# A two-layer block of mixtures, convolution and LoRA experts: lora_a in one load of longer runs, one step of x loaded later, A loaded and transposed sooner

## The reference, cut to what matters

```python
def layer0(x, cond):                                   # added to x
    h   = gelu(gelu(cond @ W0 + b0) @ W1 + b1)
    att = softmax(h @ W2 + b2)                         # 128 x 8
    o   = einsum('boi,bih->boh', einsum('bk,koi->boi', att, weight), x) + (att @ bias_k)[:, :, None]
    logits = o @ Wr.T                                  # 4 experts, the best 2 gated by a softmax
    mid = einsum('tf,erf->ter', o, A)                  # A: 4 experts x 16 x 512
    return sum_e gates[e] * (mid[e] @ B[e].T) * SCALE

def layer1(x1, cond):                                  # added to x1
    o1  = conv1d(x1, weight, 9 taps, 4 groups) + (cond @ c_weight.T)[:, :, None] + bias
    g   = relu(layernorm(o1 @ gw1.T + gb1)) @ gw2.T + gb2   # 8 experts, the best 2, capacity over all rows
    tmp = einsum('ni,eir->enr', o1, lora_A)            # lora_A: 8 experts x 512 x 16
    return o1 @ W.T + einsum('enr,ero->no', tmp * w, lora_B) / 16
```

## Time and profile before

| what | value |
|---|---|
| median of 3 runs | 302.68 us |
| the profiled execution's own time | 302.07 us |
| its span | 300.3 us |
| granted TensorE clock, mean | 0.997 |
| busy share: PE, DVE, ACT, POOL | 96%, 65%, 42%, 32% |
| moved by DMA | 52.75 MB, 176 GB/s over the span |

### The profile page before, as it was taken

How to read it: one execution, slowest core, us unless ns; L and a number is a source line. 1 busy time by engine, 2 the same in 40 slices (tenths; PEclk the granted TensorE clock), 3 DMA queues, 4 the chain that set the end, 5 groups by cost and what they waited for, 6 DMA issues and landing times.

```text
span 300.3 us, 6135 instructions
## 1 busy us (share of the span) xinstructions
PE 288.7 (96%) x1982; PEld 236.5 (79%) x1982; DVE 195.4 (65%) x506; ACT 125.3 (42%) x263; POOL 95.1 (32%) x124
## 2 busy tenths in 40 slices
PE   7999979999999999999999999999999999999994
PEld 5788957687978797879877987798777876777883
DVE  1655964743669466946594749474948555899885
ACT  3325834434622572258224822392237326103430
POOL 4361425123311431143114311431113235217660
PEclk9999999999999999999999999999999999999998
DMA  5796699893869487946794669458646790005887
GB/s 142 186 339 143 154 252 233 212 213 75 220 185 210 87 218 211 178 93 181 228 189 104 161 224 207 104 154 204 129 104 163 187 206 6 0 2 188 320 331 280
DMA packets 74400, 52.75 MB, mean 176 GB/s; under 512 B 44405, under 2 KB 61477, under 8 KB 74377
## 3 DMA queue, kind: packets, MB, share of 16 engines
q1 hardware_dynamic: 72936, 51.37, 69.1%
q10 hardware_dynamic: 1120, 1.07, 1.1%
q0 software_dynamic: 320, 0.02, 0.2%
HBM read 35.67 MB, written 16.78 MB: 175 GB/s over the span
## 4 chain that ended last, share of the span: by engine, by line
PE 54%; DMA 14%; SPq 12%; DVE 8%; issue 5%; ACT 4%; POOL 1%; DVEq 0%; ACTq 0%
PE ps_g L1139 10%; PE ps_d L1139 9%; DMA xg<-x1d 8%; PE ps_c L1277 7%; DMA x1d<-xq 7%; PE ps_a L1100 5%; PE ps_t L1293 3%; SPq L353 3%; PE ps_a L1089 3%; SPq L356 2%; ACT xq L632 2%; PE ps_d L1318 2%; PE ps_d L1319 2%; PE ps_d L1500 1%; PE ps_d L1505 1%
## 5 line engine op out<-in xcount | busy, mean ns | idle before, releaser
L512 POOL TENSOR_TENSOR o1l<-o,o1h 128x512 fp32r<-128x512 f32 x30 | 39.4, 1313 | 150.2 <-ACT o L644 150.2
L1139 PE MATMUL ps_d<-wt_hi,o1h 128*128 128x336 f32 (+1 forms) x120 | 41.1, 342 | 0.3 <-DVE y_all L961 0.3
L1139 PE MATMUL ps_d<-wt_hi,o1l 128*128 128x336 f32 (+1 forms) x120 | 38.7, 323 | 0.0
L1139 PE MATMUL ps_d<-wt_lo,o1h 128*128 128x336 f32 (+1 forms) x120 | 38.6, 322 | 0.0
L1277 PE MATMUL ps_c<-xg,cw 96*32 96x512 f32 x256 | 34.1, 604 | 3.1 <-DMA xg<-x1d 3.1
L955 DVE TENSOR_TENSOR oT<-ps_c,biasT 128x512 f32<-128x512 f32 x32 | 21.9, 686 | 22.8 <-PE ps_c L1277 21.9
L1139 PE MATMUL ps_g<-wt_hi,o1h 128*128 128x336 f32 x112 | 35.6, 318 | 0.6 <-ACT tmp_all L659 0.4
L1139 PE MATMUL ps_g<-wt_hi,o1l 128*128 128x336 f32 x112 | 35.5, 317 | 0.0
L1139 PE MATMUL ps_g<-wt_lo,o1h 128*128 128x336 f32 x112 | 35.4, 316 | 0.0
L632 ACT ACTIVATE xq<-y_all 128x512 f32 (+1 forms) x29 | 31.9, 1152 | 7.3 <-DMA x1d<-xq 4.1
L1100 PEld LDWEIGHTS ps_a<-pm,xT 128*128 128x128 f32 x256 | 30.2, 192 | 1.4 <-issue 0.8
(11 more groups left out here) (258 smaller groups left out, 577.7 us busy)
## 6 DMA issues: line engine op xcount, KB each, us to landing
xg<-x1d SPq DMA_DIRECT2D x64, 254.0 KB, 5.1
xg<-x1d SPq DMA_DIRECT2D x32, 256.0 KB, 3.8
x1d<-xq SPq DMA_DIRECT2D x30, 256.0 KB, 3.6
xs<-in_x_dram SPq DMA_DIRECT2D x6, 1024.0 KB, 6.2
out_dram<-xT SPq DMA_DIRECT2D x16, 256.0 KB, 2.1
out_dram<-xg SPq DMA_DIRECT2D x15, 256.0 KB, 2.1
y_all<-in_x_dram ACTq DMA_DIRECT2D x2, 512.0 KB, 5.2
y_all<-in_x_dram SPq DMA_DIRECT2D x1, 1024.0 KB, 5.7
```

Of the source, the lines that this page charges most:

```text
L512: pool.tensor_tensor(lo, o1[t % 2][:, :, :], hi.bitcast(fp32), ALU.subtract).then_inc(s_o1l, 1)
L1139: last = T.matmul(bank[:, 0:columns], a[:, Q - 1 - q, :], w[:, q, first:first + columns], start=(q == 0 and n == 0), stop=(q == Q - 1 and ...
```

## The change

It alters no arithmetic. (1) lora_a is loaded in one transfer: four neighbouring rows lie on one partition in DRAM already, so a run is 4 x 16 numbers (256 bytes). For that `ga` is laid out as blocks of 16 columns by q by 16, and the four places that read or write it use views of that. (2) Step 3 of x is not loaded in the setup, but in step 1 of SP's list, like those of the later steps, between the writes of step 1 and gather (1,1). (3) A and Wr are loaded ahead of the mixture's weights; PE transposes them where a `keep_busy` stood, DVE copies them to `pm` before three other instructions, and u's second product moves ahead of the transposition of B.

```diff
--- before.py
+++ after.py
@@ -29,6 +29,7 @@
     ER1 = E1 * R1
     G1 = gw1.shape[0]
     GC = G1 + ER1
+    GB = G1 // R1
     MC = (H + GC) // 2
     TAPS = convw.shape[2]
     CG = convw.shape[1]
@@ -63,6 +64,9 @@
             shape = list(v.shape)
             shape[axis] = n
             return v.broadcast_to(shape)
+
+        def blocks(v):
+            return v.rearrange("p q (e r) -> p e q r", r=R1)
 
         def wait(eng, s, value):
 
@@ -92,7 +96,7 @@
         rs = sb("rs", [P, UC])
         b_hi = sb("b_hi", [P, H], fp32r)
         b_lo = sb("b_lo", [P, H], fp32r)
-        ga = sb("ga", [P, Q, GC])
+        ga = sb("ga", [P, GC // R1, Q, R1])
         cw = sb("cw", [P, G, Q, CG])
         gw2bd = sb("gw2bd", [P, NT, E1])
         ident = sb("ident", [P, P])
@@ -331,13 +335,13 @@
             sp.dma_start(w1n, w1).then_inc(s_ld["w1"], 16)
             sp.dma_start(ctxn, ctxw).then_inc(s_ld["ctx"], 16)
             sp.dma_start(w2n, w2).then_inc(s_ld["w2"], 16)
+            sp.dma_start(aw[0:ER0], ffa.rearrange("e r h -> (e r) h")).then_inc(s_ld["aw"], 16)
+            sp.dma_start(aw[ER0:UC], ffr).then_inc(s_ld["aw"], 16)
             sp.wait_ge(s_wk0, 1)
             for j in range(4):
                 sp.dma_start(wk[C * j:C * j + K0],
                              mixw.rearrange("k (o j) i a -> j k o (i a)", j=4)[j])\
                   .then_inc(s_ld["mixw"], 16)
-            sp.dma_start(aw[0:ER0], ffa.rearrange("e r h -> (e r) h")).then_inc(s_ld["aw"], 16)
-            sp.dma_start(aw[ER0:UC], ffr).then_inc(s_ld["aw"], 16)
             sp.dma_start(mbn, row(mixb, 1, BT)).then_inc(s_ld["mixb"], 16)
             for e in range(E0):
                 sp.dma_start(bn[:, :, e * R0:(e + 1) * R0],
@@ -346,15 +350,13 @@
             sp.dma_start(wn, wmain.rearrange("(c p) h -> p c h", p=P)).then_inc(s_ld["w"], 16)
             sp.dma_start(gw1n, gw1).then_inc(s_ld["gate"], 16)
             sp.dma_start(gw2n, row(gw2, 1, NT)).then_inc(s_ld["gate"], 16)
-            for i in range(2):
-                sp.dma_start(xs[i][:, :, :], x_v[2 + i]).then_inc(s_x[i], 16)
+            sp.dma_start(xs[0][:, :, :], x_v[2]).then_inc(s_x[0], 16)
+            sp.dma_start(ga[:, GB:, :, :].rearrange("p e q r -> p e (q r)"),
+                         lora_a.rearrange("e (m q) r -> m e (q r)", q=Q)).then_inc(s_ld["lora_a"], 16)
             sp.wait_ge(s_zero, 1)
             for i in range(Q):
                 sp.dma_start(taps[i:C:Q, :, 7 - i:7 - i + TAPS],
                              convw.rearrange("o c k -> c o k")).then_inc(s_ld["conv"], 16)
-            for e in range(E1):
-                sp.dma_start(ga[:, :, G1 + e * R1:G1 + (e + 1) * R1],
-                             lora_a[e].rearrange("(m q) r -> m q r", q=Q)).then_inc(s_ld["lora_a"], 16)
 
             def write(u, t):
 
@@ -401,7 +403,7 @@
                         sp.wait_ge(s_x1w[1], (s + 1) * 16)
                     else:
                         wait(sp, s_x1w[2], (s + 1) * 32)
-                if has(s, 2) and not at_step(s, 0) and not at_step(s, 1):
+                if has(s, 2) and not at_step(s, 0):
 
                     sp.dma_start(xs[par][:, :, :],
                                  x_v[bass.ds(s + 2, 1)].rearrange("s p t h -> p (s t) h")).then_inc(s_x[par], 16)
@@ -520,8 +522,8 @@
                     mixing(1)
                     pool.wait_ge(s_gah, 1)
                     pool.wait_ge(s_gm, 2)
-                    pool.tensor_tensor(wt_lo[:, :, H:H + GC], ga[:, :, :], wt_hi[:, :, H:H + GC].bitcast(fp32),
-                                       ALU.subtract).then_inc(s_gal, 1)
+                    pool.tensor_tensor(blocks(wt_lo[:, :, H:H + GC]), ga[:, :, :, :],
+                                       blocks(wt_hi[:, :, H:H + GC].bitcast(fp32)), ALU.subtract).then_inc(s_gal, 1)
                     o1_low(0, 0)
                     return
                 if has(s, 2):
@@ -705,8 +707,8 @@
                     gate0_exp(1)
 
                     act.wait_ge(s_ss["gw1"], 1)
-                    act.wait_ge(s_ld["lora_a"], 16 * E1)
-                    nc.scalar.activation(wt_hi[:, :, H:H + GC], ga[:, :, :], ACT.Copy).then_inc(s_gah, 1)
+                    act.wait_ge(s_ld["lora_a"], 16)
+                    nc.scalar.activation(blocks(wt_hi[:, :, H:H + GC]), ga[:, :, :, :], ACT.Copy).then_inc(s_gah, 1)
                     gm_out(1)
                     u_out(2)
                     o_hi(0, 0)
@@ -833,6 +835,8 @@
             link(V.reduce_sum(sm[:, 1:2], atte, AXX))
             link(V.reciprocal(sm[:, 2:3], sm[:, 1:2]))
             V.tensor_scalar(attw[:, :, 0:K0], row(atte, 1, 4), sm[:, 2:3], None, ALU.mult).then_inc(s_ss["att"], 1)
+            dve.wait_ge(s_sp["pm"], 1)
+            V.tensor_copy(pm[:, :, :].rearrange("p c u -> p (c u)"), ps_t[:, 0:HC * UC]).then_inc(s_ss["pm"], 1)
             dve.wait_ge(s_sp["ctx"], 1)
             dve.wait_ge(s_ld["side"], 16)
             V.tensor_tensor(bex.rearrange("n (g q o) -> n g q o", q=Q, o=CG),
@@ -842,8 +846,6 @@
             dve.wait_ge(s_const, 4)
             V.tensor_tensor(attD, row(ps_v[:, 0:N0], 1, 4), row(repmask[:, :], 2, N0), ALU.mult).then_inc(s_attD, 1)
             V.tensor_copy(attT, ps_v[:, 0:P]).then_inc(s_ss["attT"], 1)
-            dve.wait_ge(s_sp["pm"], 1)
-            V.tensor_copy(pm[:, :, :].rearrange("p c u -> p (c u)"), ps_t[:, 0:HC * UC]).then_inc(s_ss["pm"], 1)
             dve.wait_ge(s_ss["pm"], 1)
             V.reduce_sum(pmsum, pm[:, :, :].rearrange("p c u -> p u c"), AXX).then_inc(s_ss["pmsum"], 1)
 
@@ -970,7 +972,7 @@
                     for t in range(NT):
                         V.tensor_copy(gw2bd[G1 * t:G1 * t + G1, t, :],
                                       ps_v[G1 * t:G1 * t + G1, Q * G1:Q * G1 + E1])
-                    V.tensor_copy(ga[:, :, 0:G1], ps_v[:, 0:Q * G1].rearrange("p (q g) -> p q g", q=Q))\
+                    V.tensor_copy(ga[:, 0:GB, :, :], ps_v[:, 0:Q * G1].rearrange("p (q e r) -> p e q r", q=Q, r=R1))\
                      .then_inc(s_ss["gw1"], 1)
                     for j in (1, 3):
                         dve.wait_ge(s_mps, 2)
@@ -1186,25 +1188,24 @@
             pe.wait_ge(s_xf, 16)
             t1(0, xs_early[0], 0)
             t1(0, xs_early[0], 1)
-            keep_busy(1)
+            pe.wait_ge(s_ld["aw"], 32)
+            pe.wait_ge(s_attd, 1)
+            for c in range(HC):
+                last = T.transpose(ps_t[:, c * UC:(c + 1) * UC], aw[:, c * P:(c + 1) * P], ident[0:UC, 0:UC])
+            last.then_inc(s_sp["pm"], 1)
             pe.wait_ge(s_ss["att"], 1)
             T.transpose(ps_v[:, 0:P], attw.rearrange("p j k -> p (j k)"), idp).then_inc(s_sp["attT"], 1)
             pe.wait_ge(s_xh, 16)
             pe.wait_ge(s_xt, 1)
             t1(0, xs_early[0], 2)
-            pe.wait_ge(s_ld["aw"], 32)
-            for c in range(HC):
-                last = T.transpose(ps_t[:, c * UC:(c + 1) * UC], aw[:, c * P:(c + 1) * P], ident[0:UC, 0:UC])
-            last.then_inc(s_sp["pm"], 1)
             pe.wait_ge(s_xt, 2)
             t1(0, xs_early[0], 3)
             pe.wait_ge(s_ss["pm"], 1)
-            u_products(0, (0,))
+            u_products(0, (0, 1))
             pe.wait_ge(s_bn, 1)
             for c in range(HC):
                 last = T.transpose(ps_t[:, c * P:(c + 1) * P], bn2[:, c, :, :].rearrange("p d e -> p (d e)"), idp)
             last.then_inc(s_sp["b"], 1)
-            u_products(0, (1,))
             pe.wait_ge(s_attD, 1)
             pe.wait_ge(s_ss["wkr"], 1)
             for o in range(MO):
@@ -1304,7 +1305,7 @@
                     wait(pe, s_y, s * NT)
                     for q in range(Q):
                         last = T.matmul(ps_g[:, 0:GC], o1[t % 2][:, Q - 1 - q, :],
-                                        ga[:, q, :], start=(q == 0), stop=(q == Q - 1))
+                                        ga[:, :, q, :], start=(q == 0), stop=(q == Q - 1))
                     last.then_inc(s_gp, 1)
 
                 def delta(u, t):
```

## The result

The change runs in 307.12 us (median of 20 executions, 303.32 to 315.66, and a single one of 1566 us that nothing here explains). The kernel before, on the same chip, has 302.17 (20 executions, 299.74 to 306.3). The ratio is 1.0151, with a 95% interval of 1.0111 to 1.0191. The forecast was 301.5, the range 299.4 to 303.3, and "slower by over 1%" had a chance of 0.04. (The ratios here leave out executions far above the quickest of their kernel; the medians don't.)

A forecast was written before the change was run, and what follows sets the result against it. PE, open 96% of the span, was taken as the bound, so only its waits count. Gain 2.9 us at conv (1,0), 1.7 given back at conv (1,1): 1.2 off 302.07 is 300.9, plus 0.61 gives 301.5; range 299.4 to 303.3.

The forecast's parts named there:

- The setup queue: SP's setup list: one lora_a load instead of eight frees SP near 24 to 26 us, needed by 27.9 for write (0,0).
- The head: Before the mixture by u: transposing A sooner brings that product (19.11) forward by 0.85 us, bounds 0 and 1.05.
- 0, if A or B lands late: Lower bound on the 0.85 us gain at the mixture by u: nothing gained when either load arrives late.
- conv (0,0): PE's first conv: with write (0,0) at 27.9, its 1.97 us wait goes; start 37.1 instead of 39.95, gain 2.85.
- The gates were late next: Step 1's gates end at 39.4, PE comes at 39.1; transposition at 39.5, gain 2.4; conv (0,1) at 42.4.
- Step 1: Gather (1,0) 3.7 us earlier, conv (1,0) gains 2.9; gather (1,1) lands at 63.15, PE waits 1.7, conv (1,1) gains 1.2.
- The 2.8: Delay in us that the moved 1 MB x load adds to gather (1,1), from 1.05 MB at 378 GB/s.
- the bound of 6.0: Upper bound in us on the x load's delay of gather (1,1), if nothing overlaps; as a rival 304.7 us, 10%.
- the clock falls: Rival: PE's clock halves in the first microseconds, where a matmul of ones goes, costing 4 us: 305.5; chance 2%.
- the 0.6 that I had added for the median: Added to the sum's 300.9: the median of the runs shown lies 0.61 us above the profiled 302.07.

## Why the prediction was wrong, step by step

*The setup queue: right, with more room than one of its reasons gives.* SP was free at 24.11, before 27.9, and write (0,0) went when its data came. But the taps took 10.26 us as they had 10.23, with 1 MB less and lora_a's load ahead of them; with 1 MB less and nothing in its place (x moved alone) they took 9.61. So the megabyte is worth little there. In the kernel with lora_a alone they end at 28.0, and that is early enough too.

*The head: wrong, +0.85 forecast, -0.2 measured.* "A is transposed before 9.2" took the load as 3 us sooner there because it was issued 3 us sooner. It had waited for that load in the kernel before as well, 0.19 us at 10.16, a row that I hadn't read. The bound "0, if A or B lands late" was the case, and below it lay a small loss that I had not put in.

*conv (0,0): right.* 38.11 for 37.1; the missing microsecond is the head's. The gates were late next, as forecast: PE waits 0.31 us for them, and conv (0,1) runs at 43.45 for 42.4.

*Step 1: conv (1,0) gained 1.9 for 2.9, and the gather (1,1) landed at 65.38 for 63.15.* This is the sum's error, and the terms can be read off. Gather (1,0) was issued 2.4 us sooner than before, not 3.7 (51.17 for 53.57), since both things that it waits for, write (1,0), landed at 51.11, and conv (0,2), done at 50.95, came later than I had them: 1.3 us. From there to the last part of gather (1,1), SP's own issues, that of x among them, took 0.65 more of the lead (56.20 for 57.95). The 1 MB made the landing 9.18 - 6.1 = 3.1 longer, where I took 2.8. In all 2.2 us, and 65.38 it is. In this execution, the quickest of its 20, the price of the load was nearly right and the queue's lead was not. But the last part of gather (1,1) took 8.29, 9.18, 10.15 and 11.26 us to land in the four profiles with the load, so the load's price runs from 2.2 to 5.2 us over the 6.1 of before. The 2.8 was near the low end of that, and the bound of 6.0 nearer than I weighed it.

*The clock: the step that failed.* The prediction charged the wait at conv (1,1) with its length, 1.7 us. I had a rival "the clock falls", but put it in the head, where PE transposes, and gave it 2%; at the one place where I myself forecast PE idle for 1.7 us, I did not ask for it. In 17 of 19 executions (the one of 1566 us aside) the mean clock shows a fall, and the median lies 3.8 us over those that kept it. Filling the wait brought 3.1 us back and the clock with it. No execution of the change with a fall was profiled; the two profiles with the same load that have one show it at conv (1,1), at 3.0 and 1.9 us, the second with a gather 2.2 us later besides. So about 3 of the 3.8 us are the clock, and the rest is most likely a longer wait. The miss adds up: 2.2 for the landing, 0.2 behind it, 3.8 between the two levels, less the 0.6 that I had added for the median, is 5.6, and 301.5 + 5.6 = 307.1.

*What stood in plain sight:* the first three times of before, 301.27 to 303.99, lay 2.7 us apart, with the profiled one at 302.07. I read that as noise. It was the same mechanism: a wait at conv (0,0), up to 2 us and more, with a fall behind it in some executions. In 99 executions of before beside the experiments, 37 had a clock of 0.996 or more and took 299.6 to 302.2 us, the rest 303.0 to 309.3. The profiled 302.07, from which the sum starts, is at the slow end of the first kind: only one of the 37 was slower. So the gain of lora_a's load is 2.4 us by the profiles (302.07 - 299.7), near the 2.0 that the forecast's terms leave without A's 0.85; but that this agrees is in part luck, since it counts from an execution that was slow for its kind. Between executions that kept the clock it is 0.55 and 1.15 us (medians, in the two groups on one chip), and by the medians of all it is 4.6: the part that I had not seen is the clock again.

## What to carry to other kernels

Price a wait of the TensorE not by its length alone: where it is as long as those behind which these profiles show a fall (1.92 to 5.08 us), add what the fall would cost, here 1.9 to 3.0 us, and look for it wherever the change creates a wait and wherever it removes one. Don't put a large load into a queue ahead of a transfer that is just in time: 1 MB ahead of a gather with 0.3 us to spare cost 2.5 to 5 us of idle PE. Nor need an earlier issue be an earlier landing: A and Wr, issued 3.1 us sooner, came at the same time. Of this change only lora_a in one load was worth keeping: 299.7 us, against 302.2 to 304.5 for the kernel before and 307.1 for the change.

## What the runs showed of the hardware

Behind or within waits of 2.36, 2.48 and 5.08 us the clock fell to half, yet the change's profiled execution kept it through 2.90, and that of before through 1.97. So one execution doesn't tell whether a wait of this size costs clock. Even the best kernel isn't free of it: in the last group its profiled execution (302.73 us) waited once, late, for a gather. Its timeline and stretches of 2 us:

```profile
155.51 1.51 PE L1280 MATMUL ps_c<-xg,cw 96*32 96x512 f32 x8 [1.92 <-DMA xg<-x1d]
```

```profile
154.00:156.00 2.00, 0.49 (x8) 0.16 (x8) 1.65 (x9) 0.00 (x0) 0.00 (x0) 1.00 0.92 163
156.00:158.00 2.00, 2.00 (x13) 1.05 (x6) 1.25 (x3) 0.38 (x2) 0.00 (x0) 0.50 0.06 16
158.00:160.00 2.00, 2.00 (x11) 2.00 (x10) 0.00 (x0) 1.08 (x2) 0.66 (x1) 0.65 0.97 242
```

After 1.92 us of idle time and half a microsecond of work the clock was at 0.50 from 156 on and back before 160, a stretch half as long as that behind conv (1,1). Where the fall comes differs too: 2.2 us after PE fell idle in the kernel with x moved alone, 2.4 after it in that of the 5.08 us, and with A alone only 1.8 us after PE had work again. And an issue can be held without its own bytes being many: lora_a's single load held SP for 0.5 to 0.9 us in the four profiles with one step of x ahead of it and for 2.0 to 2.8 in the five with two, while the taps took 10.0 to 11.0 us with one step and that load ahead of them, and 10.2 with two steps alone.
